# Third attention layer on bf16 exponentials with values in three bf16 parts; wide attention projecting its output half a step later

## The reference, cut to what matters

```python
# layer 1, "wide": 16 heads of 64, causal
qh = (q @ w_q.T).reshape(b, n, 16, 64).transpose(0, 2, 1, 3)   # kh and vh alike
scores = jnp.where(causal, einsum(qh, kh) / sqrt(64), -inf)
out = einsum(softmax(scores), vh).reshape(b, n, 1024) @ w_o.T

# layer 2: 16 heads of 8, and only the 27 queries of largest norm are kept
scores = einsum(qh, kh) / sqrt(8)
scores = scores.astype(bfloat16) + attn_mask.astype(bfloat16)
probs = softmax(scores).astype(float32)
context = einsum(probs, vh) * ps_mask        # ps_mask: top-k of sum(qh * qh)
x = x + tanh(g) * (context @ Wo.T + bo)
```

## Time and profile before

| | |
|---|---|
| median of 3 runs | 1841.23 us (1840.51 to 1841.86) |
| the profiled execution's own time | 1840.51 us |
| its span in the trace | 1838.7 us, granted clock 0.955 |
| TensorE busy | 1693.0 us (92%) |
| VectorE, ScalarE, GpSimd busy | 1084.1, 870.4, 639.9 us |
| wide attention, about | 340 to 790 us of the span |
| attention of layer 2, about | 968 to 1219 us of the span |
| GpSimd without work in the capacity stage | 800.7 to 928.0 us of the span |
| a weight load in layer 2, mean | 109 ns in L608 (float32, 32 columns), 98 ns in L584 (bf16, 128 columns) |

### The profile page before, as it was taken

How to read it: one execution, slowest core, us unless ns; L and a number is a source line. 1 busy time by engine, 2 the same in 40 slices (tenths; PEclk the granted TensorE clock), 3 DMA queues, 4 the chain that set the end, 5 groups by cost and what they waited for, 6 DMA issues and landing times. The chain is left out here.

```text
span 1838.7 us, 46448 instructions
## 1 busy us (share of the span) xinstructions
PE 1693.0 (92%) x17680; PEld 1105.1 (60%) x17680; DVE 1084.1 (59%) x2348; ACT 870.4 (47%) x2175; POOL 639.9 (35%) x1103
## 2 busy tenths in 40 slices
PE   5999959799999999867988999979999989999798
PEld 2555544577777777665775555546777755555454
DVE  5677657566666666545166676653233236777576
ACT  3555426455655655533544444434343436544354
POOL 4467508322323223300021555510000004676673
PEclk9999959899999999957999999989999989999899
DMA  4000041000000000010101000000000010000000
GB/s 114 2 2 3 2 117 35 9 7 5 8 7 5 7 7 5 2 46 6 41 0 53 2 3 3 3 2 1 1 0 0 0 35 13 2 3 3 1 24 24
DMA packets 47822, 27.64 MB, mean 15 GB/s; under 512 B 11024, under 2 KB 44560, under 8 KB 47632
## 3 DMA queue, kind: packets, MB, share of 16 engines
q1 hardware_dynamic: 42896, 24.64, 4.8%
q10 hardware_dynamic: 4736, 0.35, 0.2%
HBM read 22.88 MB, written 2.10 MB: 14 GB/s over the span
## 5 line engine op out<-in xcount | busy, mean ns | idle before, releaser
L771 DVE TENSOR_REDUCE neg_max<-scores 128x8 f32<-128x1024 f32 x192 | 235.0, 1224 | 134.7 <-PE scores L560 48.9
L1819 POOL TENSOR_TENSOR probs<-probs,inverse 128x512 f32<-128x512 f32 x128 | 133.2, 1041 | 324.6 <-DVE inverse L2022 324.5
L528 PE MATMUL scores<-k_diag,q_all 32*128 32x512 f32 x768 | 216.0, 639 | 0.9 <-DVE dropped L2158 0.9
L542 PE MATMUL turned<-q_diag,k_all 32*128 32x512 f32 x768 | 216.4, 638 | 0.0
L706 ACT ACTIVATE probs<-turned 128x1024 f32<-128x1024 f32 x128 | 131.1, 1024 | 176.5 <-PE turned L574 176.5
L412 POOL TENSOR_TENSOR k_diag<-k_all,hmask 128x512 f32<-128x512 f32 x96 | 100.0, 1043 | 324.2 <-ACT k_all L681 288.4
L1956 ACT ACTIVATE probs<-scores,neg_max 128x128 f32<-128x128 f32 x512 | 180.7, 387 | 5.3 <-DVE neg_max L2014 5.3
L1478 ACT ACTIVATE hidden_f<-hb_f,b_f 128x512 f32<-128x512 f32 x128 | 87.9, 687 | 128.7 <-PE hb_f L1425 128.4
L1434 PEld LDWEIGHTS yb_f<-w_f,hidden_f 128*128 128x128 f32 x1024 | 119.2, 192 | 14.8 <-issue 14.8
L1947 ACT ACTIVATE heads_t<-heads 128x512 f32<-128x512 f32 x64 | 38.2, 597 | 174.5 <-PE heads L1883 174.5
L1434 PE MATMUL yb_f<-w_f,hidden_f 128*128 128x128 f32 x1024 | 119.3, 275 | 0.0
(11 more groups left out here) (305 smaller groups left out, 3628.3 us busy)
## 6 DMA issues: line engine op xcount, KB each, us to landing
ctx_t<-in_ctx_t_dram SPq DMA_DIRECT2D x24, 256.0 KB, 2.9
w_f<-in_L_ffn_W_dram SPq DMA_DIRECT2D x16, 256.0 KB, 3.1
x_state<-in_x_dram SPq DMA_DIRECT2D x4, 512.0 KB, 7.6
ctx_t<-in_ctx_t_dram SPq DMA_DIRECT2D x16, 128.0 KB, 2.1
out_dram<-x_state SPq DMA_DIRECT2D x7, 256.0 KB, 2.3
w_f<-in_L_ffn_We_dram SPq DMA_DIRECT2D x1, 1024.0 KB, 7.1
taps_f<-in_L_ffn_conv_w_dram SPq DMA_DIRECT2D x1, 768.0 KB, 6.4
w_e_f<-_ffn_expert_weights_dram SPq DMA_DIRECT2D x1, 512.0 KB, 4.3
```

The lines of the kernel that those rows point to most:

```text
L528: last = nc.tensor.matmul(scores[pair][:, (g % 2) * 512:(g % 2 + 1) * 512], cols(q_all, b, S)[quad_rows(g), :], k_diag[quad_rows(g), b % 2 ...
L542: nc.tensor.matmul(turned[:, (g % 2) * 512:(g % 2 + 1) * 512], cols(k_all, b, S)[quad_rows(g), :], q_diag[quad_rows(g), b % 2, :, :].rearr ...
L771: v.tensor_reduce(neg_max[:, b % 2, 8 * pair:8 * pair + 8], scores[pair][:, :].rearrange("p (h k) -> p h k", k=S), axis=X_AXIS, op=ALU.max ...
L1819: nc.gpsimd.tensor_tensor(p4, p4, inverse[:, n % 2, CH * h:CH * h + CH].unsqueeze(2).to_broadcast([P, CH, S]), ALU.mult).then_inc(s["prob_ ...
```

## The change

In the attention of layer 2, `probs` is bf16, and the values become three bf16 tiles whose sum is the float32 value: high (ScalarE, `high_values`), the rest of it taken off (VectorE, `rest_of_values`), middle (ScalarE, `mid_values`), low (VectorE, `low_values`). They are written for a group of four items at once, spread out with zeros, so that `values_apart` of GpSimd is gone. `contexts` has 48 products where it had 16, `sums` has 16 still, with bf16 ones; each is one pass. VectorE adds the bias while it copies the values out of PSUM (`add_values`), where ScalarE copied before; two of these stand in the norms ahead of the loop and two between the rounds of `choose_first`. The tile with the three parts shares its room with the weights of earlier stages, and GpSimd clears it in `capacity_experts`.

In `attention_wide`, `project_out(n - 2)` stands after the first two productions of step n, where `project_out(n - 1)` stood at the end of the step; ScalarE does the first four exponentials before the context copy.

```diff
@@ attention_small
-        probs = sb("probs", [P, 2, 2, 8 * S])
+        probs = sb("probs", [P, 2, 2, 8 * S], BF16 if select else F32)
...
-                if real(b + 1):
+                if real(b + 1) and not select:
                     values_apart(b + 1)
...
                 for g in range(QUADS):
-                    for j in range(4):
-                        nc.tensor.matmul(heads[b % 2][32 * j:32 * j + 32, 0:S],
-                                         v_pad[:, b % 2, 128 * g + 32 * j:128 * g + 32 * j + 32],
...
+                    for k, table in enumerate(padded):
+                        for j in range(4):
+                            nc.tensor.matmul(heads[b % 2][32 * j:32 * j + 32, 0:S],
+                                             table[:, 128 * g + 32 * j:128 * g + 32 * j + 32],
...
-                                                ones_pad[:, (3 - g) * DK:(3 - g) * DK + 32],
+                                                (ones_half if select else ones_pad)[:, (3 - g) * DK:(3 - g) * DK + 32],
...
+            def high_values(c):
+                act.wait_ge(s["v_ready"], c + 1)
+                wait(act, s["sums_done"], GB * (c - 1))
+                nc.scalar.activation(part_of(c, 0), values_of(c), ACT.Copy).then_inc(s["high_done"], 1)
+
+            def mid_values(c):
+                act.wait_ge(s["rest_done"], c + 1)
+                nc.scalar.activation(part_of(c, 1), values_of(c), ACT.Copy).then_inc(s["mid_done"], 1)
...
+            if select:
+                for c in range(2):
+                    high_values(c)
             for c in range(EARLY, KV0):
                 copy_keys(c)
-                copy_values(c)
+                read["v"](c)
+            if select:
+                for c in range(2):
+                    mid_values(c)
...
+            def add_values(c):
+                dve.wait_ge(s["v_done"], c + 1)
+                v.tensor_tensor(cols(v_all, c, GW).rearrange("p (u d) -> p u d", d=D), kv_bank(c)[1].rearrange("p (u d) -> p u d", d=D),
+                                b_v[:, :].unsqueeze(1).to_broadcast([P, GB, D]), ALU.add).then_inc(s["v_ready"], 1)
+
+            def rest_of_values(c):
+                dve.wait_ge(s["high_done"], c + 1)
+                v.tensor_tensor(values_of(c), values_of(c), part_of(c, 0), ALU.subtract).then_inc(s["rest_done"], 1)
+
+            def low_values(c):
+                dve.wait_ge(s["mid_done"], c + 1)
+                v.tensor_tensor(part_of(c, 2), values_of(c), part_of(c, 1), ALU.subtract).then_inc(s["vpad_ready"], 1)
...
-                choose_first()
+                choose_first({0: lambda: add_values(2), 1: lambda: add_values(3)})
+                for c in range(2):
+                    rest_of_values(c)
+                for c in range(2):
+                    low_values(c)
@@ capacity_experts, gpsimd
+            pool.wait_ge(y_copied, 2)
+            for part in range(3):
+                nc.gpsimd.memset(st.v_parts[:, part, :, :], 0.0)
@@ attention_wide, tensor
-            for n in range(-4, NO + 1):
+            for n in range(-4, NO + 2):
                 todo = fills(n)
                 for f in todo[:2]:
                     make(f)
+                project_out(n - 2)
                 score(n + 1)
                 turn(n)
                 contexts(n - 1)
                 for f in todo[2:]:
                     make(f)
-                project_out(n - 1)
@@ attention_wide, scalar
-                context_copy(n - 1)
                 exponents(n + 1, 0)
+                context_copy(n - 1)
```

More of the change, by code:

```diff
@@ L356, in attention_small @@
                  "kdiag_ready qdiag_ready vpad_ready s0_done s1_done max0_done max1_done split spread_ready shift_turned "
-                 "shift_ready st_done exp_done sums_done inv_done heads_ready y_done x_done bq_ready mask_ready chain").split()
+                 "shift_ready st_done exp_done sums_done inv_done heads_ready y_done x_done bq_ready mask_ready chain "
+                 "high_done rest_done mid_done").split()
         s = {n: sem(n) for n in names}
@@ L381, in quad_rows, with part_of, values_of @@
             return slice(32 * g, 32 * g + 32)
+        def part_of(c, part):
+            first = c % 2 * GB * QUADS
+            return v_parts[:, part, first:first + GB * QUADS, 0:128].rearrange("p u (j c) -> p u j c", c=32)[:, :, :, 0:DK]
+        def values_of(c):
+            return cols(v_all, c, GW).rearrange("p (u j e) -> p u j e", j=4, e=DK)
         def spread_at(b, part):
@@ L400, in _ @@
             if select:
+                p.tensor_copy(ones_half[:, :], ones_pad[:, :]).then_inc(s["consts"], 1)
                 pool.wait_ge(topk["norm_done"], NG)
@@ L505, in _ @@
                 values(c)
-            if mask == "keys":
+            if mask is not None:
                 pe.wait_ge(s["consts"], 1)
-            if mask is not None:
                 pe.wait_ge(s["mask_ready"], 1)
@@ L591, in contexts @@
                 pe.wait_ge(s["exp_done"], 2 * b + 2)
-                pe.wait_ge(s["vpad_ready"], b + 1)
+                pe.wait_ge(s["vpad_ready"], b // GB + 1 if select else b + 1)
                 pe.wait_ge(s["shift_ready"], min(b + 2, NB))
                 wait(pe, s["x_done"], b - 1)
+                padded = [v_pad[:, b % 2, :]]
+                if select:
+                    first = b % (2 * GB) * QUADS
+                    padded = [v_parts[:, part, first:first + QUADS, :].rearrange("p g k -> p (g k)") for part in range(3)]
                 for g in range(QUADS):
-                    for j in range(4):
-                        nc.tensor.matmul(heads[b % 2][32 * j:32 * j + 32, 0:S],
-                                         v_pad[:, b % 2, 128 * g + 32 * j:128 * g + 32 * j + 32],
-                                         probs[:, b % 2, g // 2, ((g % 2) * 4 + j) * S:((g % 2) * 4 + j + 1) * S],
-                                         start=(g == 0), stop=(g == QUADS - 1), skip_group_check=True)
+                    for k, table in enumerate(padded):
+                        for j in range(4):
+                            nc.tensor.matmul(heads[b % 2][32 * j:32 * j + 32, 0:S],
+                                             table[:, 128 * g + 32 * j:128 * g + 32 * j + 32],
+                                             probs[:, b % 2, g // 2, ((g % 2) * 4 + j) * S:((g % 2) * 4 + j + 1) * S],
+                                             start=(g == 0 and k == 0), stop=(g == QUADS - 1 and k == len(padded) - 1),
+                                             skip_group_check=True)
             def sums(b):
@@ L722, in _ @@
                     read[kind](c)
+                if select and 2 <= b // GB + 1 < NG:
+                    if b % GB == 0:
+                        high_values(b // GB + 1)
+                    elif b % GB == 1:
+                        mid_values(b // GB + 1)
         @block.vector
@@ L759, in _ @@
                         normalise(c + 2)
+                    if c < EARLY:
+                        add_values(c)
             if mask == "pairs":
@@ L810, in _ @@
                 maximum(b + AHEAD, 1)
+                if select:
+                    for kind, c in second_fills(b):
+                        if kind == "v":
+                            add_values(c)
+                    if 2 <= b // GB + 1 < NG:
+                        if b % GB == 1:
+                            rest_of_values(b // GB + 1)
+                        elif b % GB == 2:
+                            low_values(b // GB + 1)
 class Feed:
@@ L1964, in _ @@
                     keep(f)
+                exponents(n + 1, 0)
                 context_copy(n - 1)
-                exponents(n + 1, 0)
                 for f in todo[2:]:
@@ L2158, in ranks, with ahead_of_loop @@
             v.tensor_scalar(dropped[:, 2 * half:2 * half + 2, :], above[:, :, :], -BIG, BIG, ALU.mult, ALU.add).then_inc(chosen, 1)
-        def ahead_of_loop():
+        def ahead_of_loop(between):
             read_norms(0)
@@ L2163, in ahead_of_loop @@
             read_norms(1)
+            between[0]()
             for k in range(1, rounds + 1):
                 next_eight(0, k)
+                if k in between:
+                    between[k]()
             limits(0)
```

11 lines of the change are left out of this document (8 added, 3 removed).

## The result

The changed kernel takes 1851.23 us (median of five runs, 1849.52 to 1854.63) where the kernel before takes 1841.23: 1.0063 times as long, with a 95% interval of 1.0052 to 1.0073. The forecast was 1848 with a range of 1838 to 1858.

What follows compares the result with a forecast made beforehand. TensorE was taken to bound both changed stages; wide attention +12, layer 2 steady -12.9, its late start +5.9 and lost clock +2.2 sum to +7.2, 1848 us on the median, range 1838 to 1858 for 8 in 10.

Steps and rivals of the forecast that it cites:

- Wide attention, +12: Wide attention stage: new copy stalls outweigh removed probability waits, about +0.95 us a block; +12 in all, between +8 and +16.
- v3 to k0: Wide attention: production k0 waits for VectorE's copy of v3 once the projection between them is gone; stall 0.85 us a block.
- q1 to q3: Wide attention: production q3 waits for ScalarE's copy of q1, now behind exponentials and context copy; stall 0.72 us a block.
- k1 to k3: Wide attention: production k3 waits for VectorE's copy of k1; stall 0.20 us a block.
- v0 to v2: Wide attention: production v2 waits for VectorE's copy of v0; stall 0.20 us a block.
- The rounds: Layer 2 `sums` and `contexts`: gap between bf16 product rounds taken as 0.06 us, bounds 0.057 and 0.115.
- Layer 2, steady: Layer 2 loop: shorter products gain 0.43 us a step, limited by the exponentials loop; -12.9 over thirty steps.
- the first half goes from 1.73 to 1.50: Layer 2 step, first half: time from shift to next crosswise products falls from 1.73 to the loop's least, 1.50 us.
- Layer 2, its start: +5.9 and +2.2: Layer 2 start: direct product needing key group 4 comes 5.9 us late; halved clock after the gap adds 2.2 (0 to 3).
- rival 1: Layer 2: weight loads keep bf16 rounds at 0.115 us; 1869, or halfway, steady gain gone, 1856; chance 0.20.
- rival 2: Wide attention: PSUM tiles return in time, only waits vanish; 1823, or 1838 if only ScalarE's side; chance 0.10.
- rival 3: Layer 2 start: lateness is absorbed and no clock is lost; 1842; chance 0.12.

Runs made afterwards that it cites:

- the two half changes: Changed kernel with only the projection moved in the wide attention (context copy first, as before): 1857.37 us; with only the exponentials moved (projection at its old place): 1872.45 us.
- contexts last: Changed kernel with the wide attention's contexts moved behind the remaining productions, at the end of TensorE's step: 1840.08 us, 1.0000 times the kernel before.
- the two with pairs: Changed kernel, wide attention as before, TensorE waiting for exponentials ahead of layer 2's direct products too: 1839.20 us; the same with value-split work moved off the start: 1836.66 us.
- the two mended starts: Changed kernel, wide attention as before, value-split work moved out of key group 4's way: 1836.48 us; with more of it moved into the loop: 1834.93 us.

## Why the prediction held, point by point

**Wide attention, +12.** Measured +12.2 in the stage, +0.99 a block against +0.95. Each of the four stalls, read from product to product, is the wait together with the slower pace of the stalled production, against close order: v3 to k0 measures 0.89 (forecast 0.85), q1 to q3 0.66 (0.72), k1 to k3 0.18 and v0 to v2 0.19 (0.20 each): 1.92 against 1.97. The 0.86 of waits for the probabilities are gone. Two terms that the forecast doesn't have nearly cancel: the projection takes 0.99 ahead of the masks where it took 0.89 ahead of a production, +0.4 a block, and the productions, which now stand together and ahead of the projection, follow each other more closely, -0.3. That 0.99 fits 0.95 so well is in part luck. The undone orders show that this term is the whole loss, and the two half changes that it is TensorE's order which sets VectorE's share. Right in mechanism and place, and in size but for these two.

**The rounds.** 0.057 where I took 0.06 and bounded at 0.057 and 0.115. L584 was the right row to size them by. The Trainium skill's rule, weighed in the prediction ("TensorE: Matmul & The Clock Gate", Back-to-back issue gap, 81 ns with 128 columns), does not hold for these rounds in blocks of 32 columns, twelve in a row, nor for the four products of full width that sized them (L584, 0.39 with 0.22 for the last).

**Layer 2, steady: the term that was mis-sized.** I took 0.43 a step, -12.9 in thirty. A steady step gained 0.36, and from the first to the last crosswise products the gain was 8.9 (205.7 to 196.8). The step of the working that failed is "the first half goes from 1.73 to 1.50": it goes to 1.60. I had added 0.05 to the end of the exponentials. That holds where the crosswise products come between the passes of the direct ones (1.51, with two thirds of the contexts left out), not where they come behind a second pass or behind weight loads that wait too. This is some 2 us, 0.07 a step. The other 2 are where steps are not steady. The first one grew by 0.9 (7.89 to 8.76; the last section). And the eighth to the tenth, in which the selection for the second half of the items falls, took 20.10 us where they took 20.20, so 1.0 of their gain is missing. In the first of them the output projection (L641, 1080.08) waits 0.66 us for VectorE's division (L841), ahead of which the four operations that find the selection's limit stand in the queue. They stood there before too, and TensorE came late enough not to wait. The forecast took VectorE at nothing throughout the loop. No run took this wait away.

**Layer 2, its start: +5.9 and +2.2.** First crosswise products 8.3 later against 8.1. The waiting direct product starts 36.65 us after the stage's first product where it was 30.76, 5.9 later (the working, 1008.1 less 1002.30, gives 5.8), and from it to the first crosswise products it is 8.28 where it was 5.83, 2.4 more. The idle time is 4.36 ("over 4"), the clock behind it 0.50 for some 6 us (forecast 4 to 6). The fit to a tenth is luck: six other kernels with the same start have their first crosswise products 7.3 to 8.9 later than before, 7.3 with both orders undone. Against that one, moving the steps away brings 6.1 back.

**The sum.** On the rows: 12.2 - 8.9 + 8.3, and 1.2 less after the last step, is +10.4, against +7.2 forecast and +10.0 measured on the medians. The miss of 3 is the 4.0 that is missing in the steps of layer 2, less the 1.2 behind them. The rest of the profiled execution's +14.0 is mostly the 3.7 in the gelu stage, which other kernels of this record show too (below). In rival 1, "the gain of the steady part is gone" and 1856 don't go together: without that gain the sum is +20 and the time 1861. The likeliest case happened; rival 1 and rival 2 are excluded by the rounds of 0.057 and by the stalls, rival 3 by the row at 1021.04.

## What to carry to other kernels

Work that stands between two users of a pair of buffers is the time in which a buffer is emptied. Before moving it, add up production to copy to next production, and compare with what is left between them. When products are made cheaper, first look for the loop through the other engines (here shift, exponentials, crosswise products, 1.5 to 1.6 us): what TensorE gains beyond it is waiting time, and here 32 of 48 products were nearly free. And the setting up of a cheaper form belongs in the queues' gaps inside the loop, not in one piece ahead of it: mending that was worth 5.5 us on the medians of two sessions, and 6.1 in the stage's rows (265.8 to 259.7), beside the loop's gain of 8.9.

## What the runs showed of the hardware that was not expected

**VectorE waits out a GpSimd operation that began first.** The selection's last step, at the start of layer 2, in the kernel before and then in the changed one:

```profile
1012.43 0.29 DVE L2158 TENSOR_SCALAR dropped<-above_sel 128x256 bf16<-128x256 f32 x1
1012.45 1.17 POOL L412 TENSOR_TENSOR k_diag<-k_all,hmask 128x512 f32<-128x512 f32 x1
```

```profile
1033.37 1.27 POOL L426 TENSOR_TENSOR k_diag<-k_all,hmask 128x512 f32<-128x512 f32 x1
...
1033.77 1.01 DVE L2230 TENSOR_SCALAR dropped<-above_sel 128x256 bf16<-128x256 f32 x1
1035.04 0.70 PE L541 MATMUL scores<-k_diag,q_all 32*128 32x512 f32 x2 [1.51 <-DVE dropped L2230]
...
1093.34 0.29 DVE L2230 TENSOR_SCALAR dropped<-above_sel 128x256 bf16<-128x256 f32 x1
```

Where VectorE began first it took 0.29. Where GpSimd was 0.40 ahead, the same operation took 1.01 and ended 0.14 after GpSimd's. In all ten kernels with the changed layer 2 it takes 1.01, each time 0.40 to 0.45 behind GpSimd's start, and its second execution in the changed kernel (1093.34), with no long GpSimd operation beside it, takes 0.29 again. TensorE waits for it, 1.51 where it was 0.64, and that 0.87 is the first step's 8.76 against 7.89: 0.72 from the longer operation, the rest because the selection's part before it began later, behind a bias addition. The subtraction of 1.42 us above, 0.65 elsewhere, lies beside a GpSimd operation that began 0.40 before it. No run separated the two engines here, so the cause is read, not tested. The Trainium skill has the rule ("SBUF — State Buffer", SBUF: two separate sides): the two engines share a pair of ports, for GpSimd's operations and for those of VectorE that have two inputs in SBUF or run in a mode with two ports, and who starts first holds it for the whole instruction. The subtraction has two such inputs and agrees with the rule. For `dropped`, which has one, no row shows the mode; its time agrees, but GpSimd's operation, which began first, also grew, to 1.27 where it takes 1.04 elsewhere in this loop.

**The order of kinds of products costs.** 0.09 us at each change from a production to the contexts, or from the projection to the masks, against other successors. In the rows both are changes of the tile (128\*128 to 128\*64 and to 64\*64), where a production and the projection have the same one; that this is the reason was not tested.

**A stage that nothing touches comes in two lengths.** The gelu stage takes 263.9 to 264.2 us in five of the profiled kernels (that of before, both orders undone, contexts last, and the two with pairs) and 267.5 to 267.6 in five others (changed, both half changes, and the two mended starts), 265.6 in one. In the ten microseconds behind the stage's first product the granted clock is 0.83 in the kernel before and 0.67 in the changed one. The rows don't say what decides it, and with one traced execution of each kernel they don't show both lengths in one kernel. Two single traces can so differ by 3.6 us in a stage whose code is the same.
